# Cross-attention loop of a Perceiver block: ScalarE's context copies moved behind the keys' copies

## The reference

```python
x = x + xattn(layernorm(x), ctx, ctx)      # 16 heads of 64
x = x + attn(layernorm(x))                 # 16 heads of 32, rotary positions
x = x + ffn(layernorm(x))                  # 8 experts, hidden 2048, the best 2 for each token
# in xattn:
q = query @ Wq + bq;  k = ctx @ Wk + bk;  v = ctx @ Wv + bv
attn = softmax(q k^T / 8);  out = attn v
out = out @ Wo + bo + query;  return normalized(out) * gamma + beta
```

## Time and profile before

| | us |
|---|---|
| median of 3 runs | 1748.02 (1745.85 to 1753.85) |
| profiled execution | 1757.3 |
| its span in the profile | 1755.5 |
| PE busy | 1610.5 (92%) |
| DVE busy | 1258.1 (72%) |
| ACT busy | 1011.1 (58%) |
| POOL busy | 483.7 (28%) |

### The profile page before, as it was taken

One profiled execution on the slowest core, in us unless ns is written; L12 is line 12 of the kernel. 1 busy time (PEld: TensorE's weight loads), 2 busy tenths in 40 slices (PEclk: granted clock), 3 DMA queues, 4 the chain that ended last, 5 costly groups with the idle time before them and its releaser, 6 DMA issues. The chain is left out here.

```text
span 1755.5 us, 28267 instructions
## 1 busy us (share of the span) xinstructions
PE 1610.5 (92%) x10538; PEld 1340.1 (76%) x10538; DVE 1258.1 (72%) x2234; ACT 1011.1 (58%) x1966; POOL 483.7 (28%) x429
## 2 busy tenths in 40 slices
PE   6799999999999999999999886997699999999897
PEld 6677787777777787778777775775588888888886
DVE  3677878787877887787878866677668539548852
ACT  5556676767666766677677633443556336335641
POOL 2223423333232423332331052366501102102101
PEclk9999999999999999999999998998799999999899
DMA  6720572021211212021202571111847527527721
GB/s 230 269 75 7 96 128 67 7 67 61 68 33 41 67 62 67 7 67 61 67 7 85 165 256 38 51 53 65 278 143 236 151 85 235 153 95 211 223 62 21
DMA packets 80674, 182.58 MB, mean 104 GB/s; under 512 B 28596, under 2 KB 35124, under 8 KB 79968
## 3 DMA queue, kind: packets, MB, share of 16 engines
q1 hardware_dynamic: 61488, 140.79, 23.9%
q0 software_dynamic: 19024, 39.60, 9.7%
HBM read 152.48 MB, written 64.05 MB: 123 GB/s over the span
## 5 line engine op out<-in xcount | busy, mean ns | idle before, releaser
L512 PE MATMUL psum<-ctx,Wk 128*128 128x512 f32 x1536 | 387.0, 401 | 0.0
L512 PEld LDWEIGHTS psum<-ctx,Wk 128*128 128x128 f32 x1536 | 281.5, 190 | 55.7
L1116 DVE SCALAR_TENSOR_TENSOR kT<-psum,bkc,kT 64x512 fp32r<-64x512 f32 x256 | 191.9, 750 | 107.5 <-ACT kT L1550 102.1
L512 PE MATMUL psum<-xgT,Wh 128*128 128x224 f32 (+5 forms) x1536 | 249.5, 315 | 10.6 <-issue 6.4
L512 PEld LDWEIGHTS psum<-xgT,Wh 128*128 128x128 f32 x1536 | 227.6, 196 | 28.5 <-issue 9.0
L892 PE MATMUL psum<-Wh,hs 128*128 128x512 f32 x981 | 245.6, 396 | 0.3 <-DVE hs L1391 0.3
L1560 ACT ACTIVATE Pr<-Pr,smn 128x512 f32<-128x512 f32 x128 | 92.7, 724 | 244.9 <-DVE smn L1125 244.9
L892 PEld LDWEIGHTS psum<-Wh,hs 128*128 128x128 f32 x981 | 181.1, 190 | 34.3 <-DVE hs L1391 0.7
L1741 ACT ACTIVATE gl<-psum,b1c 128x512 f32<-128x512 f32 x128 | 87.7, 686 | 201.6 <-PE psum L512 201.6
L1550 ACT ACTIVATE kT<-psum,bkc 64x512 fp32r<-64x512 f32 x256 | 174.4, 681 | 28.2 <-PE psum L512 23.3
L1123 DVE TENSOR_TENSOR Pr<-psum,Pr 64x512 f32<-64x512 f32 x256 | 176.4, 689 | 9.8 <-ACT Pr L1558 1.8
(11 more groups left out here) (194 smaller groups left out, 2635.9 us busy)
## 6 DMA issues: line engine op xcount, KB each, us to landing
raw<-in_W SPq DMA_DIRECT2D x128, 512.0 KB, 4.1
raw<-in_ctxT SPq DMA_DIRECT2D x34, 512.0 KB
expert_rows<-in_spare_rows SPq DMA_DIRECT2D x16, 1042.0 KB, 8.6
xg<-expert_rows POOLq DMA_DIRECT2D x32, 256.0 KB, 4.7
q_rows<-qst POOLq DMA_DIRECT2D x16, 256.0 KB, 4.9
qb<-q_rows SPq DMA_DIRECT2D x16, 256.0 KB, 6.5
high_parts<-Ohr POOLq DMA_DIRECT2D x32, 128.0 KB, 2.9
low_parts<-Olo POOLq DMA_DIRECT2D x32, 128.0 KB, 4.1
```

The lines of the kernel that those rows point to most:

```text
L512: mm = pe.matmul(dst, l, r, start=n == 0, stop=n == len(pairs) - 1)
L1116: v.scalar_tensor_tensor(k[other, :], bank[n % 2][own, :], bkc[own, j:j + 1], k[own, :], ALU.add, ALU.subtract).then_inc(k_lo, 1)
```

## The change

Four edits, all in the order of instructions; nothing is computed otherwise.

1. ScalarE, in the loop: the two context copies for batch b+1 no longer stand ahead of the keys' copy of turn j = 0. The first stands at the end of turn j = 0, the second at the end of turn j = 1. S1 is copied at j = 5 together with S3; S4 of batch b is copied at the end of j = 0 of batch b itself (it was at the end of j = 7 of the batch before), ahead of the first context copy.
2. VectorE, before the loop: the zeroing of `qs` stands ahead of the context's sums for batch 0.
3. At the loop's end: pieces 2 and 3 of Wo are split in turn NS-3 instead of NS-2, on ScalarE and VectorE.
4. SyncE, at the loop's end: all four pieces of Wo are loaded ahead of the output's high parts 0 and 1; high parts 2 and 3 stand behind the loads of the residuals, gamma and x1.

```diff
-            for c in range(2):
+            for c in range(4):
                 fetch(L_WO + c, wo_in[:, 2 * c:2 * c + 2, :])
             for t in range(2):
-                high_part(t)
-            for c in range(2, 4):
-                fetch(L_WO + c, wo_in[:, 2 * c:2 * c + 2, :])
-            for t in range(2, 4):
                 high_part(t)
...
             fetch_x1(0)
             fetch_x1(1)
+            high_part(2)
+            high_part(3)
...
             v.wait_ge(q_psum, 2 * NJ)
+            for r in range(2):
+                for h in range(2):
+                    own, other = slice(64 * h, 64 * h + 64), slice(64 - 64 * h, 128 - 64 * h)
+                    v.memset(qs[h][r][other, :, other].bitcast(F32), 0.0).then_inc(qbd_zero, 1)
...
-                if n in (NS - 4, NS - 2):
-                    for c in (n - NS + 4, n - NS + 5):
+                if n in (NS - 4, NS - 3):
+                    for c in (2 * (n - NS + 4), 2 * (n - NS + 4) + 1):
                         split_lo(L_WO + c, Wo[1][:, 2 * c:2 * c + 2, :], Wo[0][:, 2 * c:2 * c + 2, :])
...
-                    if j == 0 and b + 1 < B:
-                        if n:
-                            s.wait_ge(k_psum, n)
-                            s.wait_ge(v_psum, 14 * b)
-                        else:
-                            s.wait_ge(norm_out, 16)
-                        ctx_high(b + 1)
                     s.wait_ge(k_psum, n + 1)
...
-                if n < NS and b + 1 < B and j in (4, 5, 6, 7):
-                    sums_high(b + 1, (("S2", "S3", "S1", "S4")[j - 4],))
-                if n in (NS - 4, NS - 2):
-                    if n == NS - 4:
-                        s.wait_ge(v_psum, 7 * NG - 3)
-                    for c in (n - NS + 4, n - NS + 5):
+                if n < NS and b and j == 0:
+                    sums_high(b, ("S4",))
+                if n < NS and b + 1 < B and j < 2:
+                    if n == 0:
+                        s.wait_ge(norm_out, 16)
+                    elif j == 0:
+                        s.wait_ge(k_psum, n)
+                        s.wait_ge(v_psum, 14 * b)
+                    ctx_high(b + 1, j)
+                if n < NS and b + 1 < B and j in (4, 5):
+                    sums_high(b + 1, ("S2",) if j == 4 else ("S3", "S1"))
+                if n in (NS - 4, NS - 3):
+                    s.wait_ge(v_psum, 7 * NG - (4 if n == NS - 4 else 3))
+                    for c in (2 * (n - NS + 4), 2 * (n - NS + 4) + 1):
                         split_high(L_WO + c, Wo[0][:, 2 * c:2 * c + 2, :])
```

More of the change, by code:

```diff
@@ L1056, in vector_program @@
                 v.tensor_tensor(CS[name][1][:], src[:], CS[name][0][:], ALU.subtract).then_inc(s_lo, 1)
[L1057 to L1060, removed]
             def build_qbd(u):
@@ L1439, in xnT_high, with ctx_high @@
                 s.activation(xnT[0][:, :, t * P:(t + 1) * P], src, ACT.Copy).then_inc(xnT_hi, 1)
-            def ctx_high(b):
-                for c in range(2):
-                    split_high(ctx_load(b, c), ctx[b % 2][0][:, 2 * c:2 * c + 2, :])
+            def ctx_high(b, c):
+                split_high(ctx_load(b, c), ctx[b % 2][0][:, 2 * c:2 * c + 2, :])
             def weight_highs(kk):
```

## The result

The changed kernel takes 1721.15 us (median, 1718.14 to 1723.61, 4 runs) against 1749.06 us for the kernel before (1745.85 to 1753.85, 4 runs): a ratio of 0.9837, 95% interval 0.9807 to 0.9867, so 1.6% less. The forecast was 1721. Its profiled execution took 1719.35 us, with a span of 1717.5.

A forecast was written before the change was run, and what follows sets the result against it. The prediction took ScalarE's round to pace the loop after the change: 23 + 3.1 + 0.7 = 26.8 us off the profiled 1757.3 gave 1730.5, less 9.3 to the median, 1721. Its range was 1711 to 1737.

The forecast's parts named there:

- What bounds the loop: In the loop: ScalarE's own round, its fixed 1.8 us hole included, sets the pace after the change, 55.4 us a batch.
- The loop's term: In the loop: ScalarE's idle time goes, except 2 us, which gives 23 us; bounds 0 and 62.
- the 24.8: ScalarE's removable idle time in the loop: 15.8 us for keys and 9.0 us in waits for the maximum.
- the 2 us left to VectorE: In the loop: VectorE is late by a tenth or two in some turns, so 2 of 24.8 us stay.
- The clock: In the loop: fewer falls of TensorE's clock from 2.4 to 1.2 GHz expected, already counted within the 24.8 us.
- S4 later: In each batch: S4 ready at 7.6 us, a new TensorE stall of 1.0 us, hidden with 1.4 to spare, cost 0.
- The start: At the loop's start: keys' copy of turn 1 at 84.1 instead of 87.20, gain 3.1 us, bounds 0 and 5.
- The end: At the loop's end: projection starts at 995.9 instead of 996.68, 0.7 us gained; bounds 1.5 gained, 2 lost.
- A: Rival, loop: ScalarE still waits about 0.9 us a batch for TensorE, half comes back, 1734 us; chance 0.15.
- B: Rival, loop: TensorE's floor of 52.7 us a batch, loop gives 40 or more, below 1706 us; chance 0.04.
- C: Rival, loop: S4 starves TensorE, ScalarE waits 4 us a batch for keys, slower, 1775 us; chance 0.05.
- D: Rival: only start and end gain, the loop's removed waits become waits for the maximum, 1744 us; chance 0.06.

The follow-up runs named there:

- e7: The changed kernel with GpSimd instead of ScalarE copying the high parts of S1 to S4 for batches 1 to 15: 1708.57 us, ratio 0.9757.
- e10: The kernel before with edits 2, 3 and 4 alone, ScalarE's loop order as before: 1751.02 us, ratio 0.9997.
- e8: e4 with one added wait that holds back GpSimd's first context sum of a batch by some 1.8 us: 1735.80 us, ratio 0.9895.
- e4: The changed kernel with both context copies together at the end of turn j = 0: 1746.28 us, ratio 0.9970.
- e5: The changed kernel with the context copies ahead of the keys' copies of turns j = 0 and 1: 1741.69 us, ratio 0.9958.
- e3: The changed kernel with the sums' copies (S1, S4) back at their old places, only the context copies moved: 1724.59 us, ratio 0.9837.
- e6: The changed kernel with S4 copied behind both context copies at the end of turn j = 0: 1758.30 us, ratio 1.0044.
- e1: The changed kernel with the zeroing of qs put back behind the context's sums: 1720.45 us, ratio 0.9823.
- e2: The changed kernel with the loop's end as before (Wo split in turn NS-2, loads in the old order): 1721.92 us, ratio 0.9831.
- e11: e7 with the context copies at the ends of turns j = 1 and 5, GpSimd's second low part behind the sums: 1703.67 us, ratio 0.9719.

## Why the prediction was right, and where its sizes were off

**What bounds the loop.** Right: ScalarE's round, with its fixed hole of 1.8 us in each turn. Between 107 and 916 us that hole is its only wait after the change (214.2 us, 118 times), and e7, which takes instructions off ScalarE and none off TensorE, shortens the period by 1.14 us.

**The loop's term** (23 us) was right by the medians and 6 too small by the profiles. By the medians 27.9 less 3.2 and 0.6 leave 24. By the profiles the loop gave 29.4: all of the 24.8 listed, and some 4 us in turn j = 2 (7.18 became 6.90, 14 times 0.28) that are in no list of waits, because the next keys' copy starts only 0.28 us late there. Part of the difference to the medians is that one execution: e10, with the same order in the loop and profiled at 1751.8 us, near its median, needs 4 us less for the same 14 batches, and its clock falls in 8 of them instead of 10. The rest of the difference stays open. The term that was off is the 2 us left to VectorE: it kept nothing. A turn of 6.6 to 7.1 us leaves it time, and the trace of e8 suggests that 5.63 does not. The period came out 0.3 us lower than the 55.4 forecast.

**The clock** was named and left inside the 24.8, and that was the right sum, but it hides how the gain comes. Two neighbouring batches of the kernel before, the first without a fall and the second with one (length, busy time of PE, PEld, DVE, ACT and POOL, granted clock, DMA):

```profile
322.01:378.07 56.06, 53.54 (x357) 43.13 (x356) 45.68 (x82) 39.82 (x81) 18.05 (x15) 1.00 0.16 53
378.07:435.39 57.32, 54.82 (x358) 44.57 (x357) 45.69 (x82) 40.04 (x81) 18.07 (x15) 0.97 0.16 52
```

All batches without a fall take 56.06 us, so the order itself gives 56.06 - 55.12 = 0.94 us a batch, 13 us in 14. With the 1.9 us of copies that the batch ahead of turn 120 lacks, the 14 batches gave 14 x (57.08 - 55.12) + 1.9 = 29 us; the other 16 lie in the ten batches in which the clock falls to 1.2 GHz behind the idle stretch of TensorE. Eight of them cost 1.2 us each. The one of 59.8 us also holds the long division at 209 us, so some 2.5 of the 16 are that and not the clock. This split is worked out from rows. A loop without falls is not enough for the gain: e4 and e5 have none in these 14 batches and are within 0.5% of the kernel before. What makes the clock fall in one batch and not in the next, with the same waits, stays open.

**S4 later** (cost 0, stall 1.0 us at 7.7): right. It is 0.76 us at 7.67, and e3, which undoes it, is not faster. The spare time was finite, as e6 shows.

**The start** (3.1 us): 3.2 in the profile, to the keys' copy of turn 1. The working gave it to the keys' copy and the zeroing together. e10 shows that the zeroing alone gives none of it; e1, without the zeroing, has lost 0.5 us of it by turn 1 and 3.4 by turn 3, most of that with the clock down, though its time is not longer.

**The end** (0.7 us): 0.8 by the trace of e2; by the times it can't be seen. That the transposes, and not Wo, come last was right too.

**The rivals.** A (half comes back, 1734) would have needed waits of ScalarE for keys; there is none. B (the floor of TensorE) is out of this change's reach, since ScalarE's hole stays, and is reached nearly by e11; the floor was 0.8 us a batch too low, 52.7 against the 53.5 for which TensorE is busy there. C is what e6 makes, at 1758 and not 1775. D (start and end only) took 4 us for them, and e10 shows that they alone give nothing. What the prediction did not see is that the new place of the context's copies mattered by 1.3 to 1.7 us a batch against its neighbours e5 and e4; the change put the copies clear of a collision with GpSimd that the working never mentioned, and that was luck. It costed them by ScalarE's own time alone, 0.95 us each, and those 0.95 us were right only in the place that the change chose.

## What to carry to other kernels

When two engines are busy in turns and both wait, lay their rounds beside each other turn by turn: the gain is the idle time that comes from uneven extras, and it stops at the fixed hole of the slower round. When a copy is moved, follow what it releases on GpSimd, and look what VectorE does at that moment; a 0.5 us instruction that becomes 1.5 us in one turn of each batch shows only with the durations of one form listed one by one. A shorter turn is no gain if the third engine can't end its list in it.

## What the runs showed of the hardware

A division on VectorE of 128x512 from and to SBUF took 0.49 us alone and 1.52 us when it began 0.07 us after a GpSimd addition of 1.30 us, which kept its length; with the addition held back it took 0.49 us again (e4 against e8). Between turns 8 and 120 the clock fell in 10 of 14 batches of the kernel before and in 8 of e10, where TensorE has one idle stretch of 1.8 us in each batch, and in 11 of e6, with one of 2.7 us. It did not fall in the changed kernel, in e4 or in e5, whose longest such stretches are 0.8 to 0.9 us, nor in e7 and e11, which have none above 0.5 us.
